# Reordering a deformable-sampling and pooling kernel: prologue, warming matmuls, layer 1, and one early pair of offset columns

## The reference, cut to what matters

```
x = x + L0(gn(x))
  offsets = conv3x3(x, off_w) + off_b      # 8 heads x 9 taps x (x, y)
  aw = sigmoid(conv3x3(x, attn_w) + attn_b) # 8 heads x 9 taps
  v = Wv x                                  # 1x1
  sampled = bilinear samples of v at (pixel + offset), 9 taps a head
  out = Wo (sum over taps of aw * sampled)
x = x + L1(gn(x))
  p1 = relu(conv3x3(x, p1_w) + p1_b);  pool1 = running maximum upwards
  p2 = relu(conv3x3(x, p2_w) + p2_b);  pool2 = running maximum leftwards
  p_gn1 = group_norm(conv3x3(pool1 + pool2, p_w));  gn1 = group_norm(conv1x1(x, c1_w))
  out = relu(conv3x3(relu(p_gn1 + gn1), c2_w) + c2_b)
```

## Time and profile before

| | us |
|---|---|
| timed runs | 142.09, 140.74, 142.00 (median 142.0) |
| profiled execution, its own time | 142.17 |
| its span | 140.2 |
| busy in the span: TensorE, VectorE, ACT, POOL | 121.3, 99.5, 63.9, 34.3 |
| chain that ended last: TensorE, VectorE, issue, ACT | 42%, 29%, 12%, 6% |
| VectorE's largest wait: parts L839 for cells L1114 | 12.3 in 7 waits |

### The profile page before, as it was taken

The page is one execution under the profiler, slowest core; times in us unless marked ns, Lnnn a source line. Parts: engine busy times, 40 slices in busy tenths (PEclk is TensorE's granted clock), DMA queues, the critical chain, the costliest instruction groups (busy, mean ns, idle before and its releaser), DMA issues.

```text
span 140.2 us, 3079 instructions
## 1 busy us (share of the span) xinstructions
PE 121.3 (87%) x1252; PEld 101.7 (72%) x1252; DVE 99.5 (71%) x211; ACT 63.9 (46%) x130; POOL 34.3 (24%) x49
## 2 busy tenths in 40 slices
PE   3999859986899989999899989997879997979770
PEld 3687659975899879997898869775557664647450
DVE  6559996282898398985999379978472879692620
ACT  3979698539945586046952057100400452040100
POOL 8950003209201800018000594050030010111000
PEclk9999986999999999999999999999999999999998
DMA  2930000066899995200000000000000000000033
GB/s 84 237 51 0 0 0 5 0 169 142 194 229 212 219 185 118 64 0 0 0 0 5 0 0 0 0 5 0 2 0 5 5 5 0 0 5 0 8 71 77
DMA packets 8078, 7.34 MB, mean 52 GB/s; under 512 B 4734, under 2 KB 6944, under 8 KB 8064
## 3 DMA queue, kind: packets, MB, share of 16 engines
q1 hardware_dynamic: 7456, 6.62, 21.6%
q10 hardware_dynamic: 608, 0.52, 1.5%
HBM read 2.22 MB, written 0.52 MB: 20 GB/s over the span
## 4 chain that ended last, share of the span: by engine, by line
PE 42%; DVE 29%; issue 12%; ACT 6%; DMA 3%; SPq 3%; POOL 1%; POOLq 1%; DVEq 0%; ACTq 0%
PE bank L1080 9%; DVE part L839 7%; PE bank L1125 6%; PE bank L1068 6%; PE bank L1103 4%; DVE prod L831 4%; DVE vd L951 3%; DMA w_v_s<-in_w_v 3%; PE bank L1245 3%; PE bank L1212 3%; PE bank L1041 2%; DVE part L801 2%; PE bank L1114 2%; DVE pooled L957 2%; DVE bn L671 2%
## 5 line engine op out<-in xcount | busy, mean ns | idle before, releaser
L839 DVE TENSOR_TENSOR part<-vd,bank 128x512 f32<-128x512 f32 (+2 forms) x25 | 19.6, 831 | 13.2 <-PE bank L1114 12.3
L831 DVE TENSOR_TENSOR prod<-hat,prod 128x576 f32<-128x576 f32 (+2 forms) x25 | 21.3, 918 | 3.0 <-ACT hat L563 3.0
L1025 PE MATMUL bank<-ones_r 128*128 128x512 f32 x72 | 19.9, 430 | 2.1 <-POOL w_pair L413 2.1
L1125 PE MATMUL bank<-cst,part 128*128 128x128 f32 x168 | 20.3, 273 | 0.8 <-DVE part L839 0.8
L1125 PEld LDWEIGHTS bank<-cst,part 128*128 128x128 f32 x168 | 18.6, 140 | 1.9 <-DVE part L839 1.7
L1025 PEld LDWEIGHTS bank<-ones_r 128*128 128x128 f32 x72 | 14.5, 208 | 5.2 <-POOL w_pair L413 2.1
L1103 PE MATMUL bank<-cst,prod 128*128 128x128 f32 x144 | 17.4, 272 | 0.8 <-ACT vd L505 0.8
L1103 PEld LDWEIGHTS bank<-cst,prod 128*128 128x128 f32 x144 | 16.1, 140 | 1.2 <-ACT vd L505 0.9
L1080 PE MATMUL bank<-w_cross,g_cross 128*128 128x432 f32 (+1 forms) x90 | 16.7, 337 | 0.3 <-DVE w_cross L814 0.3
L326 POOL TENSOR_TENSOR prod<-prod 128x640 f32<-128x640 f32 (+1 forms) x5 | 6.4, 1274 | 41.5 <-DVE prod L831 41.5
L1080 PEld LDWEIGHTS bank<-w_cross,g_cross 128*128 128x128 f32 x90 | 15.4, 205 | 0.9 <-issue 0.4
(11 more groups left out here) (103 smaller groups left out, 184.9 us busy)
## 6 DMA issues: line engine op xcount, KB each, us to landing
vd<-vd SPq DMA_DIRECT2D x2, 840.0 KB, 9.2
vd<-vd SPq DMA_DIRECT2D x2, 784.0 KB, 14.7
vd<-vd SPq DMA_DIRECT2D x2, 300.0 KB, 4.7
prod<-in_w_off SPq DMA_DIRECT2D x1, 486.0 KB, 5.9
vd<-vd SPq DMA_DIRECT2D x2, 224.0 KB, 4.8
w_s<-in_w SPq DMA_DIRECT2D x4, 72.0 KB, 6.4
wc_s<-in_wc SPq DMA_DIRECT2D x2, 144.0 KB, 4.1
wp_s<-in_wp SPq DMA_DIRECT2D x4, 72.0 KB, 2.4
```

The costliest lines, as they stand in the source:

```text
L831: return nc.vector.tensor_tensor(cells[:, STEP0[i]:STEP0[i] + n], hat[:, c % 2, at + 3:at + 3 + n, 0:ck].rearrange("p d (k s) -> p d k s", ...
L839: return nc.vector.tensor_tensor(to.rearrange("p d (q e) -> p d q e", e=HD), moved_by, weights.unsqueeze(3).to_broadcast([P, n, cx, HD]), ...
L1025: nc.tensor.matmul(ps.rearrange("p (a q) -> p a q", q=P), ones_r[:, :], ones_r[:, :].unsqueeze(1).to_broadcast([P, 4, P]), start=True, sto ...
L1125: last = nc.tensor.matmul(comb_bank[:, j * P:(j + 1) * P], part[:, n % PARTS, d, j * P:(j + 1) * P], ident, start=(m == 0 and d == 0 and j ...
```

## The change

- Prologue: TensorE no longer waits on `u_ready` before the first pair of chunk 1. ACT copies the first half's values before it makes chunk 0's row hats, and chunk 1's offsets before the second half's values.
- Pairs: (2,0) goes ahead of chunk 0's tap sums (it stood ahead of its first row sum), (2,1) ahead of chunk 0's first row sum (it stood ahead of the third), (3,1) ahead of chunk 1's third row sum (it stood ahead of chunk 2's tap sums).
- Warming matmuls: 4 instead of 16 ahead of chunk 3, 3 instead of 10 ahead of chunk 4.
- Parts: in chunks 2 to 4 the base part is made third and the part of row displacement 1 last.
- Layer 1: the norms of the first half's pooled convolution and the second half's skip convolution change places in number and so in POOL's order; VectorE does the second half's pools before the first half's skip affine, and the first half is finished before the second half's skip affine; ACT takes the halves in turn; the group means stand at other taps.

```diff
--- before.py
+++ after.py
@@ -66,21 +66,20 @@
 BASE0 = 16
 CELLS = 21
 GROUPS = ((0, 8, 2), (8, 16, 5))
-APPLY = ((0,), (1,), (2,), (3, 4))
-TERMS = (4, 4, 4, 4, 5)
+APPLY = (((0,), (1,), (2,), (3, 4), ()),) * 2 + (((0,), (1,), (), (3, 4), (2,)),) * 3
 VCOLS = W + 3
 PIECES = (0, 5, VCOLS)
 RANGES = ((0, 4), (4, 9), (9, PW))
 DVE_IMAGES = (N, N // 2, N)
 LOW_TAPS = (0, 2, KS)
-BEFORE = (0, 0, 1, 0, 0)
-BETWEEN = ((0, 2), (0,), (0,), (), ())
-WARM_LOAD, WARM_START, WARM_CHUNK = 11, 26, (0, 0, 0, 16, 10)
+BEFORE = (1, 0, 0, 0, 0)
+BETWEEN = ((0,), (0, 2), (0,), (), ())
+WARM_LOAD, WARM_START, WARM_CHUNK = 11, 26, (0, 0, 0, 4, 3)
 WARM_IN = (5, 4, 0)
 PARTS = 5
 
 
-G0, G_IN, G_C1, G_P, NORMS = 0, 1, 3, 5, 7
+G0, G_IN, G_C1, G_P, NORMS = 0, 1, (3, 5), (4, 6), 7
 
 
 C_GB = 0
@@ -296,8 +295,8 @@
             return ap.rearrange("p (y x) -> p y x", x=W)
 
         def group_stats(s):
-            b, q = {G0: (7, 0), G_IN: (5, 0), G_IN + 1: (4, 0), G_C1: (2, HW), G_C1 + 1: (6, HW), G_P: (0, HW),
-                    G_P + 1: (4, HW)}[s]
+            b, q = {G0: (7, 0), G_IN: (5, 0), G_IN + 1: (4, 0), G_C1[0]: (2, HW), G_C1[1]: (6, HW), G_P[0]: (0, HW),
+                    G_P[1]: (4, HW)}[s]
             return bank[b][:, q:q + 3 * HALF]
 
         def cell_blocks(c, g):
@@ -585,12 +584,12 @@
             sizes_and_modulation(0)
             row_distances(0)
             copy_high(2)
+            copy_values(0)
             row_hats(0)
-            copy_values(0)
             short_of(0)
             steps_x(0)
+            copy_offsets(1)
             copy_values(1)
-            copy_offsets(1)
             sizes_and_modulation(1)
             for c in range(NC):
                 if c:
@@ -623,28 +622,27 @@
                                      bias=b12_s[lo, 0:1]).then_inc(r12_ready, 1)
 
             def affine_c(g):
-                act.wait_ge(norm_ready, g + 2)
+                act.wait_ge(norm_ready, G_C1[g] - 1)
                 for r in range(2):
                     last = nc.scalar.activation(c_aff[:, DUO * g + r, :], pair_banks(C1_BANK[g])[:, r],
-                                                ACT.Identity, bias=ab[:, G_C1 + g, 3, r:r + 1],
-                                                scale=ab[:, G_C1 + g, 2, r:r + 1])
+                                                ACT.Identity, bias=ab[:, G_C1[g], 3, r:r + 1],
+                                                scale=ab[:, G_C1[g], 2, r:r + 1])
                 last.then_inc(caff_ready, 1)
 
             def second_input(g):
                 n = DUO * g
                 act.wait_ge(pre_ready, n + 1)
                 nc.scalar.activation(inner(g2, n, 1)[:, 0], rows_cols(pre[:, n, :]), ACT.Relu,
-                                     bias=ab[:, G_P + g, 3, 0:1]).then_inc(g2_ready, 1)
+                                     bias=ab[:, G_P[g], 3, 0:1]).then_inc(g2_ready, 1)
 
             act.wait_ge(ld_vec, 32)
             act.wait_ge(x1_ready, 1)
             nc.scalar.activation(x1_b, x1[:, :, :], ACT.Identity, bias=vec_s[:, 4:5]).then_inc(x1_b_ready, 1)
             branches(0)
             branches(1)
-            affine_c(0)
-            affine_c(1)
-            second_input(0)
-            second_input(1)
+            for g in range(2):
+                affine_c(g)
+                second_input(g)
             for n in range(1, HALF, 2):
                 act.wait_ge(res_ready, n + 1)
                 for half, rows in enumerate((lo, hi)):
@@ -887,15 +885,17 @@
                 if c == NC - 1:
                     ve.wait_ge(prod_ready, ND * NC)
                     window_test()
-                for m, rows in enumerate(APPLY):
+                for m, rows in enumerate(APPLY[c]):
                     if c and m == 2:
                         residual(c - 1)
-                    apply_steps(rows)
-                if c == NC - 1:
-                    ve.wait_ge(flag_ps, 1)
-                    link(nc.vector.tensor_reduce(vtotal[:, :], bank[1][0:1, 0:2 * NC], AX_X, ALU.add))
-                    nc.vector.tensor_copy(vcount[:, :], vtotal[:, :]).then_inc(flag_sb, 1)
-                apply_bases()
+                    if c == NC - 1 and m == ND - 1:
+                        ve.wait_ge(flag_ps, 1)
+                        link(nc.vector.tensor_reduce(vtotal[:, :], bank[1][0:1, 0:2 * NC], AX_X, ALU.add))
+                        nc.vector.tensor_copy(vcount[:, :], vtotal[:, :]).then_inc(flag_sb, 1)
+                    if rows:
+                        apply_steps(rows)
+                    else:
+                        apply_bases()
 
             def window_test():
                 ve.wait_ge(far_test, NC)
@@ -937,7 +937,7 @@
 
             def c1_stats(g):
                 ve.wait_ge(c_ps, g + 1)
-                norm_stats(G_C1 + g, [pair_banks(C1_BANK[g])[:, r] for r in range(2)])
+                norm_stats(G_C1[g], [pair_banks(C1_BANK[g])[:, r] for r in range(2)])
 
             def reverse(ap):
                 n = ap.ap[-1][1]
@@ -960,16 +960,16 @@
 
             def p_stats(g):
                 ve.wait_ge(p_ps, g + 1)
-                norm_stats(G_P + g, [pair_banks(P_BANK[g])[:, r] for r in range(2)])
+                norm_stats(G_P[g], [pair_banks(P_BANK[g])[:, r] for r in range(2)])
 
             def c1_affine(g):
-                affine(G_C1 + g, DUO, vec_s[:, 2:3], vec_s[:, 3:4], vec_s[:, 1:2])
+                affine(G_C1[g], DUO, vec_s[:, 2:3], vec_s[:, 3:4], vec_s[:, 1:2])
 
             def both_branches(g):
 
-                s = G_P + g
+                s = G_P[g]
                 affine(s, DUO, vec_s[:, 0:1])
-                ve.wait_ge(norm_ready, s - G_C1 + 2)
+                ve.wait_ge(norm_ready, s - 1)
                 ve.wait_ge(caff_ready, g + 1)
                 for r in range(2):
                     nc.vector.scalar_tensor_tensor(pre[:, DUO * g + r, :], pair_banks(P_BANK[g])[:, r],
@@ -989,17 +989,17 @@
 
             c1_stats(0)
             pools(0)
-            group_variance(G_C1)
+            group_variance(G_C1[0])
+            pools(1)
+            p_stats(0)
             c1_affine(0)
-            pools(1)
+            group_variance(G_P[0])
             c1_stats(1)
-            p_stats(0)
-            group_variance(G_C1 + 1)
-            group_variance(G_P)
+            both_branches(0)
+            group_variance(G_C1[1])
             c1_affine(1)
-            both_branches(0)
             p_stats(1)
-            group_variance(G_P + 1)
+            group_variance(G_P[1])
             both_branches(1)
             ve.wait_ge(neg_ready, 1)
             ve.wait_ge(x1_b_ready, 1)
@@ -1061,7 +1061,7 @@
 
                 for ready in (g_high, g_shifted):
                     pe.wait_ge(ready, ranges_for(CHUNKS[c][0] + 2 * b + KS))
-                if c and b == 0:
+                if c > 1 and b == 0:
                     pe.wait_ge(u_ready, c)
                 for i, (x, to, kx) in enumerate(fed_by(c, b)):
                     for t in range(2):
@@ -1117,7 +1117,7 @@
 
             def row_sum(c, m):
 
-                w, nd = CHUNKS[c][1], TERMS[m]
+                w, nd = CHUNKS[c][1], sum(STEPS_X[i][1] for i in APPLY[c][m]) or ND
                 n = ND * c + m
                 pe.wait_ge(part_ready, n + 1)
                 for d in range(nd):
@@ -1252,11 +1252,11 @@
             pe.wait_ge(ld_wp, 64)
             for g in range(2):
                 pe.wait_ge(g1_ready, DUO * (g + 1))
-                branch_conv(g, {4: G_C1} if g else {})
+                branch_conv(g, {4: G_C1[0]} if g else {})
                 skip_conv(g)
             pool_conv(0, {})
-            pool_conv(1, {2: G_C1 + 1, 4: G_P})
-            out_conv(0, {4: G_P + 1})
+            pool_conv(1, {2: G_P[0], 5: G_C1[1]})
+            out_conv(0, {2: G_P[1]})
             out_conv(1, {})
```

## The result

The changed kernel takes 136.27 us (median of 4 runs, 135.66 to 136.41), the kernel before 142.05 in the same comparison; the ratio is 0.9615 with a 95% interval of 0.9542 to 0.9688. The forecast was 135.7 us in a range of 134.8 to 137.9. The profiled execution took 136.41 us, its span 134.5, against 142.17 and 140.2: 5.76 us less where the sum said 6.5.

A forecast was written before the change was run, and what follows sets the result against it. The prediction saw four places where the engine carrying the chain, TensorE or VectorE, idles or does useless work. Layer 0's 5.45 us (5.05 - 0.4 + 0.7 + 0.1) plus layer 1's 1.05 made 6.5; 142.17 - 6.5 = 135.7 us, range 134.8 to 137.9.

The forecast's parts named there:

- The start of pair (1,0), 3.0 us: Prologue: chunk 1's first pair starts 1.35 us sooner and, keeping its clock, saves 1.65 us more; 3.0 us in all.
- its bounds, 1.35 and 3.0: Prologue gain: 1.35 us from the earlier start alone, 3.0 us if the half clock behind the idle time goes too.
- the first rival: The half clock stays, or comes once somewhere else; a stretch costs 1.65 us, giving 137.3 us; chance 0.2.
- The pair ahead of the tap sums, 2.55 us left of 3.0: Chunk 0: with pair (2,0) first, VectorE becomes the bound; chunk 1's tap sums start at 41.95 instead of 44.52.
- Fewer warming matmuls: Chunk 3: with four instead of 16, tap sums start at 73.25 instead of 78.32, a gain of 5.05 us.
- The base part third, -0.4: Chunk 3: VectorE, there at 79.35, waits for POOL's last base sum at 79.71; loss 0.4 us, bounds 0 and 0.8.
- the wait in chunk 4, +0.7: Chunk 4: with three warming matmuls instead of ten, VectorE's 0.71 us wait for its cells goes; gain 0.7 us.
- Layer 1, 1.05 us: Layer 1: scans come 1.12 us sooner, the last output convolution starts at 130.6; gain 1.05 us, bounds 0 and 1.07.
- The new wait of 1.3 us: Layer 1: TensorE stands 1.3 us for the group mean inside the first output convolution.
- The second: Rival: layer 1 gives nothing, as the group mean at the third tap makes TensorE wait; 136.8 us, chance 0.12.
- the third: Rival: the warming matmuls were needed; TensorE falls to 1.2 GHz in chunks 3 and 4; 146.7 us, chance 0.04.
- the fourth: Rival: chunk 3's early tap sums don't come, as something else holds them; 2.5 us not gained, 138.2 us, chance 0.04.

The follow-up runs named there:

- a_wait: Changed kernel with TensorE's wait on u_ready ahead of chunk 1's first pair put back: 139.37 us.
- b_start: Kernel before, without TensorE's wait on u_ready ahead of chunk 1's first pair and nothing else of the change: 140.10 us, ratio 0.9781.
- b_fill: Kernel before with 7 warming matmuls in the 1.94 us idle time ahead of chunk 1's first pair, the wait kept: 141.02 us, ratio 1.0035.
- a_pairs: Changed kernel with pairs (2,0), (2,1) and (3,1) where they stood in the kernel before: 136.02 us.
- a_warm: Changed kernel with 16 and 10 warming matmuls ahead of chunks 3 and 4 again, instead of 4 and 3: 140.09 us.
- a_apply: Changed kernel with the base part last in all chunks, as before: 136.41 us.
- a_layer1: Changed kernel with layer 1 in the order of the kernel before: 138.19 us.
- a_nowarm: Changed kernel without any warming matmul ahead of chunks 3 and 4: 136.49 us.
- a_pairs_in: Changed kernel with the pairs where they stood before and 7 instead of 4 warming matmuls between the two group means ahead of layer 1: 134.92 us, ratio 0.9565.
- a_in: Changed kernel with 7 instead of 4 warming matmuls between the two group means ahead of layer 1 only: 136.31 us, ratio 0.9557.
- best: Changed kernel with the edits of a_pairs, a_apply and a_in together: 134.23 us, ratio 0.9414.

## Why the prediction was right, and where it was off

The direction, the place of each gain and most sizes were right; the sum was 0.7 us too large against the profiled execution and 0.6 against the median. Of the 0.74 us, 0.54 are the late start; layer 0 gave 0.58 less than summed and layer 1 0.29 more, so two errors in part made up for each other.

- *The start of pair (1,0), 3.0 us:* from the bias matmul, the second values end 2.86 us sooner (the start itself 1.24 of it). Shown by a_wait and b_start, 2.86 and 2.95 for layer 0. But the choice between its bounds, 1.35 and 3.0, was argued from one trace, and the executions beside b_fill refute the certainty in it: 1.65 of it exists only in executions where the clock fell before (the first rival had suspected as much). Between executions with a whole clock the two kernels stand at about 140.65 and 136.06, 4.6 us apart, not 5.8; the sum without the 1.65 says 4.85. So the size of the difference of medians depends on how often the kernel before meets its half clock, and here it had met it in the profiled execution that the forecast started from.
- *The pair ahead of the tap sums, 2.55 us left of 3.0:* **the step that failed in size.** "VectorE's first part starts at 33.7, 0.6 before 34.28"; it came at 34.79 - 0.54 = 34.25. The copy and the transpose back were set at 0.55 us and take 0.83 (the first block ends at 32.81 + 1.15 = 33.96, the part begins at 34.79), the block of nine itself takes 1.15 where 1.05 was put down (the earlier trace rows has 1.20), and the tap sums began 0.2 us later than summed. Chunk 1's tap sums gained 44.52 - 43.07 + 0.54 = 1.99. The mechanism, VectorE becoming the bound and TensorE waiting 1.1 us, is there with 1.14. The sum let this step take 0.45 us of the prologue's 3.0; a_pairs shows a cost of 1.42: without the early pair chunk 1's tap sums come 3.34 us sooner than in the kernel before (24.46 against 27.80), with it 1.99.
- *Fewer warming matmuls:* 5.05 us at chunk 3's tap sums, measured 78.32 - 74.50 + 0.54 = 4.36. The step itself, 2.5, is 4.36 - 1.99 = 2.37; all the rest is the 0.56 carried along. a_warm gives 2.72 for both chunks together.
- *The base part third, -0.4, and the wait in chunk 4, +0.7:* VectorE waited 0.24, and the 0.71 us are gone. From chunk 3's tap sums to the last residual 0.51 were gained where 0.4 were summed. a_apply gives 0.3 for the order.
- *Layer 1, 1.05 us:* measured 1.34; a_layer1 1.32. The new wait of 1.3 us is there with 1.28. The group mean came 26.81 us after the last residual instead of 28.14, where 1.12 less was summed.
- *The late start,* -0.54 us in this execution, is in no step.

Of the rivals, the first (a half clock stays or comes somewhere else) is no second case but a share of the executions; a stretch costs 1.5 to 1.7 us in layer 1's distances (32.22 to 32.43 against 30.75). The new idle time of 1.28 us in layer 1, which it named, had no half clock behind it: in all ten traces that have that wait the 56 matmuls behind it take 3.25 us. The second falls with a_layer1, the third with a_nowarm, the fourth with the trace. The Trainium skill's rule (page "TensorE: Matmul & The Clock Gate", section "Part 1: The HAM clock gate") that activity releases the throttle agrees with a_pairs_in, a_in and best, whose 18 executions all stayed at 0.992 or more, but b_fill, filled at another place, still has 6 of 12 at 0.988 or less. As an argument for the warming matmuls in chunks 3 and 4 the rule decided nothing: in a_nowarm's trace TensorE keeps its clock there without them.

What stays open: undoing the parts one at a time gives 2.86 + 2.72 - 1.42 - 0.29 = 3.87 for layer 0, not 4.87. ACT's new order, which no kernel undid alone, has 0.49 of the missing 1.0 by the first part (14.71 in b_start, 14.22 in a_pairs, which differ ahead of it in that order alone), and it is still 0.50 at chunk 2's tap sums (41.93 and 41.43). The rest of the way from b_start to a_pairs, 3.32 - 0.50 = 2.82, is the fewer warming matmuls and the order of the parts together, where undoing each in the kernel after gives 2.72 - 0.29 = 2.43; this interplay was not separated. The late start, and why one execution's clock falls and the next one's does not, were not tried either.

## What to carry to other kernels

Work pulled ahead of a stage is free only if no other engine waits for that stage: here a pair of 3.4 us of TensorE put in front of VectorE's input cost 1.4 us in the end, and put behind those tap sums it no longer did. Matmuls without use cost nearly their whole length where the next thing in the queue is ready (12 more of them, 2.75 us, delayed chunk 3's tap sums by 2.48) and nothing in idle time; what they are worth there is not shown beyond the 18 executions that kept their clock. Where the times of one kernel spread by more than a step is worth, undo the step and compare the distance between two rows of the trace, started at a row ahead of the change.

## What was not expected of the hardware

The half clock comes in stretches that may or may not occur in an execution of the same program: 17 executions of the kernel before on one chip have mean clocks of 0.964 (1), 0.975 or 0.976 (5), 0.986 or 0.988 (2) and 0.994 to 0.998 (9), with times of 145.0, 143.4 to 143.8, 141.8 to 142.5 and 140.2 to 141.4 us, some 1.4 us a step.

VectorE's first multiplication of chunk 0 (hats by modulation, 128x720) took 0.91 us before and 1.05 here. Rows of VectorE and POOL:

```profile
25.26 1.05 DVE L873 TENSOR_TENSOR prod<-hat,mod 128x720 f32<-128x720 f32 x1 [1.68 <-ACT hat L556]
```

```profile
24.66 0.88 POOL L441 TENSOR_TENSOR vd<-vd 128x320 f32<-128x320 f32 x1
29.46 2.11 POOL L441 TENSOR_TENSOR vd<-vd 128x832 f32<-128x832 f32 x1 [3.92 <-ACT vd L504]
```

POOL's subtraction (0.88 us, with two inputs) is now in flight when it starts; before, it came 1.5 us behind. In b_start the two overlap as well, and there VectorE's small edge operation takes 0.98 us instead of 0.30 and POOL's 1.26 instead of 0.87:

```profile
25.34 0.98 DVE L880 CUSTOM_DVE_ANT_0 edge<-hat 128x144 f32<-128x144 f32 x1
```

```profile
24.91 1.26 POOL L442 TENSOR_TENSOR vd<-vd 128x320 f32<-128x320 f32 x1 [0.38 <-ACT vd L505]
```

In b_fill the edge operation takes 0.98 us again (25.18 to 26.16), beside a POOL subtraction of the usual 0.87 that started first (25.12 to 25.99).

The Trainium skill (page "SBUF — State Buffer", section "SBUF: two separate sides", under "Who interferes with whom") says that a VectorE instruction with two SBUF inputs contends with a GpSimd one that reads SBUF, that whichever issues first has the shared pair of ports for its whole length, and that the other waits. The rows agree with it in the main: the edge operation, issued second, ends 0.15 us behind POOL's in b_start and 0.17 in b_fill, and POOL's is longer in b_start, where it starts 0.52 us before VectorE's multiplication (24.52 to 25.43) ends; in b_fill it starts 0.14 us before that end and is not longer. In a_wait, where nothing overlaps, the two VectorE operations take 0.91 and 0.30 us. Behind them VectorE still waits for ACT's hats (0.36 us in the kernel after and in b_start), so they cost nothing here; no run was made that changes the overlap alone.
